# Other slots for the routing's steps inside the third attention of a fused transformer

## The reference, cut to what matters

```python
x = x + _L2_xattn_ref(_layernorm(x), ctx_1024, ctx_1024, mask, ...)
# _L2_ffn_ref(_layernorm(x), wg, w1, b1, w2, b2):
cap = ceil(1.0 * 2 * N / 8)
gvals, gidx = top_k(softmax(xt @ wg), 2); gvals = gvals / gvals.sum(-1)
for kk in range(2):                       # place in the expert's list
    m = one_hot(gidx[:, kk], 8)
    loc = cumsum(m, axis=0) - 1 + offset; offset = offset + m.sum(axis=0)
    keep = loc at the chosen expert < cap
disp[expert, place] += x * keep           # rows sent to the experts
```

## Time and profile before

| | us |
|---|---|
| median of three executions | 4146.7 (4140.27 to 4158.86) |
| the profiled execution | 4131.01 |
| its span, first to last instruction | 4128.9 |
| third attention, groups 0 to 15 | 1404.3 to 2026.5 of the span |
| rest of the routing, to the last indirect DMA | 2026.5 to about 2083 |
| PE, DVE, ACT, POOL busy, share of the span | 84%, 83%, 58%, 37% |

### The profile page before, as it was taken

One profiled execution on the slowest core, in us unless ns is written; L12 is line 12 of the kernel. 1 busy time (PEld: TensorE's weight loads), 2 busy tenths in 40 slices (PEclk: granted clock), 3 DMA queues, 4 the chain that ended last, 5 costly groups with the idle time before them and its releaser, 6 DMA issues. The chain is left out here.

```text
span 4128.9 us, 95016 instructions
## 1 busy us (share of the span) xinstructions
PE 3458.1 (84%) x31907; PEld 2505.8 (61%) x31907; DVE 3417.6 (83%) x6484; ACT 2382.1 (58%) x4440; POOL 1545.5 (37%) x935
## 2 busy tenths in 40 slices
PE   6983979998599788888568839989499998899999
PEld 3553647766477465565456627667366666677777
DVE  7888879999799788878755579889788888788888
ACT  2431657776277466655545527667576665466665
POOL 1210035553000345555444435545155563122222
PEclk9985989999599899989788969999699998899999
DMA  2001322222100222222121142222222222000000
GB/s 65 14 25 64 130 50 64 66 61 53 42 1 0 50 56 55 60 56 56 52 76 57 58 127 64 59 60 58 64 58 48 53 57 77 24 16 15 15 10 16
DMA packets 161066, 209.96 MB, mean 51 GB/s; under 512 B 38044, under 2 KB 110048, under 8 KB 157857
## 3 DMA queue, kind: packets, MB, share of 16 engines
q1 hardware_dynamic: 151457, 187.83, 16.8%
q0 software_dynamic: 8192, 16.92, 1.2%
q10 hardware_dynamic: 1152, 1.57, 0.2%
HBM read 53.09 MB, written 42.21 MB: 23 GB/s over the span
## 5 line engine op out<-in xcount | busy, mean ns | idle before, releaser
L1102 ACT ACTIVATE a_p<-a_p 128x480 f32<-128x480 f32 x832 | 501.7, 603 | 528.5 <-DVE a_p L939 521.8
L698 POOL TENSOR_TENSOR a_km<-a_k,a_slots 96x1920 fp32r<-96x1920 f32 x186 | 631.3, 3410 | 184.9 <-DMA a_k<-a_kh 181.2
L934 DVE TENSOR_REDUCE a_mx<-a_sc 128x4 f32<-128x480 f32 (+1 forms) x832 | 540.6, 650 | 129.8 <-PE a_sc L1206 106.4
L939 DVE TENSOR_TENSOR a_p<-a_sc,a_mx 128x480 f32<-128x480 f32 x832 | 531.8, 639 | 19.7 <-DVE a_mx L934 0.5
L1108 ACT ACTIVATE a_pt<-a_tp 120x512 f32<-120x512 f32 x832 | 485.4, 584 | 104.0 <-PE a_tp L1215 101.6
L1215 PE MATMUL a_tp<-ident,a_p 128*120 128x128 f32 x3328 | 518.9, 280 | 6.1 <-ACT a_pt L1108 6.1
L1200 PE MATMUL a_sc<-a_km,a_qr 96*128 96x480 f32 x768 | 403.5, 525 | 103.0 <-DVE a_p L939 71.5
L1215 PEld LDWEIGHTS a_tp<-ident,a_p 128*120 128x120 f32 x3328 | 414.7, 141 | 84.8 <-issue 37.2
L1239 PE MATMUL a_nd<-a_pt,a_vm 120*32 120x128 f32 x6656 | 297.6, 285 | 19.2 <-ACT a_pt L1108 18.8
L1200 PEld LDWEIGHTS a_sc<-a_km,a_qr 96*128 96x128 f32 x768 | 149.0, 194 | 210.4 <-issue 116.6
L2196 ACT ACTIVATE f_s<-f_pu 128x512 f32<-128x512 f32 x256 | 153.5, 600 | 212.4 <-PE f_pv L1678 212.4
(11 more groups left out here) (455 smaller groups left out, 8840.3 us busy)
## 6 DMA issues: line engine op xcount, KB each, us to landing
a_qr<-a_qh SPq DMA_DIRECT2D x372, 64.0 KB, 2.0
a_k<-a_kh SPq DMA_DIRECT2D x384, 60.0 KB, 2.0
a_ctx<-in_ctxT SPq DMA_DIRECT2D x64, 240.0 KB, 2.7
a_qr<-a_ql SPq DMA_DIRECT2D x186, 64.0 KB, 2.0
a_k<-a_kl SPq DMA_DIRECT2D x192, 60.0 KB, 2.0
dispatched<-f_empty SPq DMA_DIRECT2D x8, 1040.0 KB, 20.9
f_xr<-dispatched SPq DMA_DIRECT2D x32, 260.0 KB, 2.6
chosen<-f_none SPq DMA_DIRECT2D x8, 1024.0 KB, 11.8
```

What stands on the lines that cost most here:

```text
L698: v.tensor_tensor(KM[par][:, i, :, :].rearrange("p b (j k) -> p b j k", k=KN), K3[:, i, :, :].unsqueeze(2).to_broadcast([TR, GB, 4, KN]), ...
L934: v.tensor_reduce(mx[:], view, AX.X, ALU.max).then_inc(mx_ready, 1)
L939: v.tensor_tensor(PR[s % 4][:].rearrange("p (h k) -> p h k", k=k), view, mx[:].unsqueeze(2).to_broadcast([P, heads, k]), ALU.subtract).the ...
L1102: a.activation(PR[s % 4][:], PR[s % 4][:], ACT.Exp).then_inc(exp_ready, 1)
```

## The change

No operation of the batch is added or removed. The steps are issued in other slots; "odd 9" is slot 9 of group 2b+3.

| step | before | after |
|---|---|---|
| DVE Newton steps | odd 4, 5, 6, 7, one in each | odd 3 (one, behind L350 to L353), 4 (two), 5 (one) |
| ACT `HL`, first and second group | odd 7-8, odd 10-11 | odd 5-6, odd 12-13 |
| PE transposes | odd 9, odd 11 | odd 10, odd 15 |
| ACT `HS` | odd 9, odd 11 | odd 9, odd 14 |
| PE logits | odd 10, odd 12 | odd 12, even 3 |
| ACT `L` | odd 10, odd 12 | odd 11, even 2 |
| DVE choices | odd 13 to even 1 | even 4 to 8 |
| ACT exponential | even 2 | even 8 |
| DVE weights, places, copies | even 4, 6 to 9, 10 | even 9, 10 to 13, 14 |
| PE counts | even 5 | even 10 |
| ACT rows of the first group | even 5-8 | even 10-13 |
| POOL, first indirect DMA of the batch | even 13 | even 15 |

(The table gives DVE's slots for the batches after the first, whose statistics begin in slot 1, since the copies for the batch before take slot 0.) Between transposes and logits PE now also gives up the bank and takes it again (`held`, `take_bank`, `after_main`), and `uses` checks the order of three pairs of uses in place of two.

```diff
@@ vector
             for n in range(4):
-                yield
+                if n % 2 == 1:
+                    yield
                 dve.wait_ge(self.chain, done)
...
-            yield from self.at("dve", self.GROUPS * b + 3, 13)
+            yield from self.at("dve", self.GROUPS * b + 4, 4)
             dve.wait_ge(self.l_ready, self.GROUPS * (b + 1))
...
-            yield from self.at("dve", self.GROUPS * b + 4, 4)
+            yield from self.at("dve", self.GROUPS * b + 4, 9)
...
-            yield from self.at("dve", self.GROUPS * b + 4, 6)
+            yield from self.at("dve", self.GROUPS * b + 4, 10)
...
-                yield from self.at("dve", g + 4, 10 - 10 * (g % self.GROUPS))
+                yield from self.at("dve", g + 4, 14 - 14 * (g % self.GROUPS))
@@ scalar
-                yield from self.at("act", self.GROUPS * b + 3, 7 + 2 * i)
+                yield from self.at("act", self.GROUPS * b + 3, 5 + 7 * i)
...
-                yield from self.at("act", self.GROUPS * b + 3, 9 + 2 * i)
+                yield from self.at("act", self.GROUPS * b + 3, 9 + 5 * i)
...
-                yield
+                self.uses[1] += 1
+                yield from self.at("act", self.GROUPS * b + 3, 11 + 7 * i)
                 act.wait_ge(self.lg_done, g + 1)
...
-            yield from self.at("act", self.GROUPS * b + 4, 2)
+            yield from self.at("act", self.GROUPS * b + 4, 8)
...
-                yield from self.at("act", g + 4, 5 - 5 * (g % self.GROUPS))
+                yield from self.at("act", g + 4, 10 - 10 * (g % self.GROUPS))
@@ tensor
-                yield from self.at("pe", self.GROUPS * b + 3, 9 + 2 * i)
+                yield from self.at("pe", self.GROUPS * b + 3, 10 + 5 * i)
...
-                yield
+                self.held = (self.hs_ready, g + 1)
+                yield from self.at("pe", self.GROUPS * b + 3, 12 + 7 * i)
                 pe.wait_ge(self.hs_ready, g + 1)
+                self.take_bank(pe)
+                self.after_main(pe)
...
-            yield from self.at("pe", self.GROUPS * b + 4, 5)
+            yield from self.at("pe", self.GROUPS * b + 4, 10)
@@ gpsimd
-            yield from self.at("pool", g + 4, 12 - 12 * i)
+            yield from self.at("pool", g + 4, 14 - 12 * i)
```

More of the change, by code:

```diff
@@ L297, in __init__ @@
         self.main_last = None
-        self.uses = [0, 0, 0, 0]
+        self.uses = [0] * 6
     def at(self, engine, group, slot):
@@ L480, in scalar @@
                              ACT.Copy).then_inc(self.l_ready, 1)
-                self.uses[1] += 1
-            yield from self.at("act", self.GROUPS * b + 4, 2)
+                self.uses[5] += 1
+            yield from self.at("act", self.GROUPS * b + 4, 8)
             act.wait_ge(self.d_ready, b + 1)
@@ L530, in tensor @@
                 last.then_inc(self.lg_done, 1)
+                self.uses[4] += 1
                 self.held = (self.l_ready, g + 1)
-            yield from self.at("pe", self.GROUPS * b + 4, 5)
+            yield from self.at("pe", self.GROUPS * b + 4, 10)
             pe.wait_ge(self.ones_ready, 2 * b + 2)
@@ L2357, in unit @@
             return n // HB // (NT // E) * HB + n % HB
-        assert route.uses[0] == route.uses[1] and route.uses[2] == route.uses[3], (route.uses, route.now)
+        assert all(route.uses[n] == route.uses[n + 1] for n in (0, 2, 4)), (route.uses, route.now)
         route.now = dict.fromkeys(route.now, 10 ** 6)
```

## The result

The changed kernel takes 4167.0 us (median of 9 runs, 4160.3 to 4193.5) where the kernel before takes 4146.7 (9 runs). The ratio is 1.0062, 95% interval 1.0039 to 1.0084: slower by 20 us, where I had forecast 13 us faster and a range that ended at 4160.

The account below looks back on a forecast made before the run. PE and VectorE both bound a bare group; routing added waits, PE work and holds. Terms -56.6 + 12.6 + 29 - 2 + 4.1 = -13 us took the median from 4146.7 to 4134 us, range 4106 to 4160.

Parts of the forecast that it names:

- The baseline: Whole kernel: the profiled execution goes from 4131 to 4118 us, the median, 15.7 above it, from 4146.7 to 4134.
- the L520 waits: Third attention, mainly odd slots 9 to 13: spacing PE's transposes from their rows removes 56.6 us of VectorE waits; bounds -57 to -28.
- Where could they be replaced?: Ring slots: ScalarE may wait for what PE makes one slot later, under 0.66 us of transposes; put at nothing.
- a lower granted clock: Even slots 12 to 15: a lower clock following VectorE's holds could make PE late; left out, no size given.
- the term of PE's work: Odd slots 10, 12, 15 and even 3: transposes and logits cost 1.8 us, seven times, +12.6; bounds 0 and 24.
- Holds: Even groups 4 to 14: GpSimd's running instructions hold VectorE 9.3 us, not 4.4; +4.9 each, +29 over six; bounds 0 to +69.
- The rule: Routing steps: a VectorE instruction with two SBUF inputs, or in 2-port mode, waits until the whole GpSimd instruction ends.
- Odd and even groups: Third attention pairs: odd group falls from 45.5 to 38 us, even group rises from 37 to 42.
- Rival C: Ring slots: new ScalarE and PE waits replace the old, +62 us, 4196; signs: waits above 1, odd groups above 41; chance 0.12.
- Newton's steps: Odd groups: twelve small VectorE instructions either way in two slots fewer; put at nothing.
- GpSimd's queue: Groups' slots 0 to 3: late products make PE 1 to 2 us late, absorbed but for a few tenths.
- The rest: Batch 6's first choice leaves group 15, -2 us; after the attention, choices, logits and copy add +4.1; nothing else can change.

## Why the prediction was wrong

**The baseline.** "The profiled execution would go from 4131 to 4118; the median of the runs shown, 15.7 above it". I carried these 15.7 us along as a constant. They hid a mechanism: two of three profiles of the kernel before have some 100 late semaphores and a third attention 19 to 20 us longer, the one that I read has none.

**The step that failed first** is "So the L520 waits and with them the 56.6 us should go". The L520 waits went; the time didn't. In the profile after, VectorE waits 82.2 us. "Where could they be replaced?" was answered with ScalarE alone and put at nothing, but late semaphores put new waits into even slots 2 and 6 (2.5 and 1.4 us a group) and lengthen those of slot 0 of both kinds of group by 0.5 and 0.9. Against plain DMAs the lateness costs 631.6 - 608.4 = 23 us in the kernel before and 639.1 - 605.3 = 34 in the changed one. I had laid GpSimd's DMAs beside VectorE's instructions only, never beside PE's; in the trace that I had, nothing would have shown. The prediction's sentence on a lower granted clock did not name the cause of these waits: they follow the DMAs.

**The size of that term.** With plain DMAs VectorE's waits go from 41.6 + 22.2 = 63.8 us (kernel before, groups 2 to 15) to 37.3: -26.5, where -56.6 + 12.6 = -44 were forecast. Some 9 of the 17.5 are missing because these waits were 63.8 and not 72.7 to begin with. Of the 37.3 that are left, some 12 are new, 1.2 and 0.8 us a group in even slots 0 and 4, behind PE's transposes of odd 15 and its logits of even 3: the term of PE's work, +12.6, had its size. The rest stays in the odd groups, above all in slots 8, 12 and 13, which wait 2.9 us a group even so: PE's transposes, the logits and the values' projection are still close there. Without the new ones the ring's waits fell by 38.5, where 56.6 were forecast and -57 to -28 given as bounds.

**Holds.** Forecast +4.9 us for each even group; with plain DMAs they go from 4.6 to 8.5, +3.9, and in odd groups from 4.7 to 4.0. The rule held, and nearly its size.

**Odd and even groups.** Forecast 38 and 42. Without indirect DMAs 38.8 and 42.8, a pair of 81.6 where the kernel before so altered has 81.4: the change moves 5.8 us from the odd group to the even one. The third attention gains 3 us, where the terms that lie in it make -17 (-56.6 + 12.6 + 29 - 2). With the waits at -26.5, the holds at 6 x 3.9 - 7 x 0.7 = 18.5 and the -2 as forecast the sum is -10. The other 7 us are in no term. Groups 9 and 10 show where they may be, the clock (first the changed kernel, then the kernel before, both with plain DMAs; PEclk is the figure 0.88 or 1.00):

```profile
1772.40:1815.30 42.90, 34.54 (x397) 24.27 (x396) 40.77 (x81) 23.81 (x49) 28.85 (x40) 0.88 0.21 54
```

```profile
1779.90:1815.60 35.70, 28.89 (x383) 20.16 (x382) 34.39 (x75) 21.84 (x45) 18.94 (x21) 1.00 0.23 59
```

The even group 10 was at full clock before and is no longer; the odd group 9 goes from 0.89 to 0.91 only, and PE is 1.5 us longer busy in the pair. So the mechanism that the prediction's last sentence names as left out is there, but that it costs the 7 us isn't shown.

**Rival C**, the other side, did not decide. ScalarE waits for L522 13 times, 14.7 us, longest 2.1, against 6.6 us before, over the 1 us that was named as its sign; but the odd groups kept below 41, the other sign. The time came out near C's region by another mechanism.

**Newton's steps** at nothing: the profile agrees, the timed runs don't. They give 15.8 us for this step alone, so it may be a second term that failed, and it is the largest open end of the account.

**GpSimd's queue.** "PE is late by 1 to 2 us there" in even slot 3: not so; with plain DMAs the low part of the keys came 8.1 us into the even group, and VectorE waited nowhere over 1.2 us for scores.

**The rest.** "Only the third attention and what follows it of the routing, 1404 to 2083 us, can change" is a step that failed too: 16 instructions more on PE slowed a later loop. By the means of the profiles the fourth attention goes from 463.5 to 470.4 us, +7; with the 240 waits in both it is equal, and 16 of the 20 us remain. In the profiles of these two kernels the third attention is 6.6 us longer with the change (632.8 to 626.2) and the rest of the routing 5.9 (2.8 by the means of the others; +4.1 was forecast). From the last indirect DMA to the fourth attention, where the change touches nothing, the profiles of all kernels take 349 to 367 us. The ends of such sums are single executions that spread by 10 us and more, so the division of the 20 us is good to some 5 us.

## What to carry to other kernels

Before the profile of one execution is used as a baseline, set it against the spread of the runs: if it lies well off the median, a mechanism may be missing from it, and a second profile can show it. Where several engines hand work round in a ring, count the waits that stay when the steps are spaced, from the neighbours in the same slots, and not only those that go. A wait that the view puts down to a DMA that the instruction doesn't read is a lead: look for the semaphore that it needs, and for what ran beside its sender. Compare loops that a change does not touch as well: their instructions may be fetched at other moments.

## What the runs showed of the hardware

- With indirect DMAs of GpSimd under way PE's semaphores came up to 2.9 us late (5 to 7 us where six to ten DMAs followed each other), and several then within 0.1 us of each other. With plain DMAs to fixed places and iotas instead, in two kernels (one execution each), none came late. It appears above all where the DMA meets the values' matmuls (66 and 32 late ones when the DMAs were kept away from them, 87 to 149 in the others that had any); in one execution of the kernel before it did not appear.
- A VectorE instruction held by GpSimd isn't always let in when GpSimd's current instruction ends: 8.22 us through the low part of the queries and two products, and 7.27 through two products. The Trainium skill ("SBUF — State Buffer", section Who interferes with whom) has the lock for the whole instruction; the holds in the earlier trace rows agree, these two last longer than one instruction.
- A loop's speed depended on instructions added ahead of it: fourth attention 442 to 443 us with 240 waits more on PE (with 240 idle waits in the kernel before, no instruction packet from the third pair on), 483 with 16 more and 9 packets of 16 KB in each slow pair, 455 to 471 in three profiles of the kernel before. Which numbers of instructions make it slow is open.
